# A vision-transformer block on one core: max scores from the spread q and k, and a new order of all engines' work

## What is computed

```python
h = concat([cls_tok, cls_token, patches @ W_lin.T + b_lin])      # 198 rows of 192 per image
# attention: 12 heads of 16, q scaled by 16**-0.5, rotary on q and k
q, k, v = split(layernorm(h) @ w_qkv.T)
h = h + softmax(rope(q * scale) @ rope(k).T) @ v @ w_proj.T + b_proj
# feed-forward: weights ternary, activations rounded to 8 bits after rmsnorm
u = quant(rmsnorm(layernorm(h)) * g_in) @ ternary(w_in).T        # 192 -> 2 * 512
y = silu(gate) * up
h = h + quant(rmsnorm(y) * g_out) @ ternary(w_out).T             # 512 -> 192
```

## Time and profile before

| | us |
|---|---|
| median of 3 runs | 1232.6 |
| lowest and highest run | 1226.38, 1236.34 |
| the profiled execution, its own time | 1228.96 |
| span from the first to the last instruction in it | 1227.2 |
| mean granted clock of TensorE in it | 0.986 |

### The profile page before, as it was taken

One profiled execution on the slowest core, in us unless ns is written; L12 is line 12 of the kernel. 1 busy time (PEld: TensorE's weight loads), 2 busy tenths in 40 slices (PEclk: granted clock), 3 DMA queues, 4 the chain that ended last, 5 costly groups with the idle time before them and its releaser, 6 DMA issues.

```text
span 1227.2 us, 36712 instructions
## 1 busy us (share of the span) xinstructions
PE 1175.8 (96%) x12229; PEld 839.3 (68%) x12229; DVE 960.5 (78%) x2335; ACT 870.0 (71%) x1736; POOL 890.6 (73%) x1605
## 2 busy tenths in 40 slices
PE   6699999999999999999999999999999999999887
PEld 5566766776767767767776776776776776766556
DVE  3455787887788888888888888888888888888786
ACT  1145677777677777777777777777777787778686
POOL 3755687877677787777787777777777788776354
PEclk9889999999899999999999999999999999999899
DMA  7434433443334443444434434344343444322010
GB/s 199 138 94 112 112 95 95 130 117 94 108 96 119 118 120 91 117 127 111 124 89 120 114 99 113 91 130 108 109 122 93 117 122 114 90 80 71 28 50 29
DMA packets 201611, 129.17 MB, mean 105 GB/s; under 512 B 55114, under 2 KB 200725, under 8 KB 201333
## 3 DMA queue, kind: packets, MB, share of 16 engines
q1 hardware_dynamic: 198852, 123.70, 37.2%
q10 hardware_dynamic: 2576, 3.14, 1.0%
HBM read 66.57 MB, written 10.70 MB: 63 GB/s over the span
## 4 chain that ended last, share of the span: by engine, by line
PE 80%; DMA 6%; DVE 5%; ACT 3%; issue 2%; SPq 2%; POOL 2%; ACTq 0%; POOLq 0%; DVEq 0%
PE turn L535 15%; PE score L593 12%; PE turn L615 10%; PE turn L553 10%; PE turn L644 6%; PE score L573 5%; PE turn L602 5%; DMA qkT<-nmaxT 4%; PE turn L623 3%; DVE nmax L935 3%; PE turn L561 2%; PE turn L662 2%; PE turn L624 2%; PE turn L517 2%; PE turn L545 2%
## 5 line engine op out<-in xcount | busy, mean ns | idle before, releaser
L935 DVE TENSOR_REDUCE nmax<-score 99x8 f32<-99x1584 f32 x192 | 347.3, 1809 | 165.3 <-PE score L573 165.3
L744 ACT ACTIVATE prob<-score 99x1584 f32<-99x1584 f32 x192 | 286.4, 1492 | 95.4 <-PE score L593 95.1
L535 PE MATMUL turn<-wlin,xp 128*128 128x192 f32 x1188 | 228.0, 344 | 8.0 <-DMA xp<-in_x 8.0
L535 PEld LDWEIGHTS turn<-wlin,xp 128*128 128x128 f32 x1188 | 198.9, 197 | 18.1 <-issue 8.8
L593 PE MATMUL score<-qkT 32*99 32x198 f32 x3072 | 179.2, 347 | 12.8 <-DVE nmax L935 7.7
L615 PE MATMUL turn<-prob,vaug 99*32 99x198 f32 x3072 | 168.3, 338 | 0.0
L1122 POOL TENSOR_TENSOR yg<-early,gout 128x512 f32<-128x512 f32 x99 | 125.8, 1271 | 46.9 <-ACT yr L808 41.5
L593 PEld LDWEIGHTS score<-qkT 32*99 32x99 f32 x3072 | 116.1, 161 | 56.0 <-issue 39.3
L553 PE MATMUL turn<-wqkv,xT 96*128 96x384 f32 x396 | 151.7, 506 | 0.0
L767 ACT ACTIVATE xiT<-turn 96x256 bf16<-96x256 bf16 x99 | 37.5, 379 | 128.6 <-PE turn L633 128.4
L615 PEld LDWEIGHTS turn<-prob,vaug 99*32 99x32 f32 x3072 | 80.9, 109 | 63.7 <-issue 37.1
(11 more groups left out here) (94 smaller groups left out, 2406.1 us busy)
## 6 DMA issues: line engine op xcount, KB each, us to landing
xp<-in_x SPq DMA_DIRECT2D x63, 588.0 KB, 5.1
qkT<-qkd SPq DMA_DIRECT2D x84, 192.0 KB, 2.5
tab<-joined SPq DMA_DIRECT2D x98, 112.0 KB, 2.7
orec<-rden_kept SPq DMA_DIRECT2D x192, 49.5 KB
out<-h SPq DMA_DIRECT2D x99, 96.0 KB, 3.0
onum<-osb SPq DMA_DIRECT2D x64, 99.0 KB, 2.6
vaug<-vt SPq DMA_DIRECT2D x30, 148.5 KB
onum<-osb SPq DMA_DIRECT2D x64, 49.5 KB, 2.3
```

Of the source, the lines that this page charges most:

```text
L535: last = pe.matmul(turn[:, k, 0:D], xp[:, c, place:place + TILE], wlin[:, c, :], start=(c == 0), stop=(c == KC - 1))
L744: act.activation(prob[:, :, 4 * g:4 * g + 4, :].rearrange("p t r n -> p r t n"), score[0:TT, :, 0:2 * TOKENS].rearrange("p r (t n) -> p r ...
L935: dve.tensor_reduce(nmax[:, b % 2, :, g:HEADS:GROUPS].rearrange("p t r -> p r t"), score[0:TT, :, 0:2 * TOKENS].rearrange("p r (t n) -> p ...
```

## The change

- `max_scores` reads `qkT` itself, seen as fp32r (`bitcast`). `qkTr`, `round_qkT` and its semaphore are gone; TensorE waits for the landing of the last two tiles' `place_qk`.
- The tables: max scores at `2 * final_tile(b) + 10` (the same numbers as before), the output half a step later (`OUT_AT`), projections at `(OUT_AT - 3) // 2`; two labels later in the step lists of what follows them.
- The order of calls in the step is rewritten on all five engines, with other offsets. The weights of the feed-forward are loaded from ACT at `SUM_STEP - 8` = 2 and summed at 8, scaled at 11, rounded at 13 and 14.
- `take` gives `ffn_in` an aligned pair of banks (0 and 1 or 2 and 3).

The unchanged loops and helper functions are as before. The diff, without the removal of `Q_COPIES` and of the semaphore:

```diff
@@ -74,11 +74,11 @@
...
-            top.append(max(top[-1] + 1 if top else 0, 2 * (final_tile(b) + 4) + 2))
+            top.append(max(top[-1] + 1 if top else 0, 2 * final_tile(b) + 10))
         turn.append(top[-1])
         for g in range(GROUPS):
             soft.append(max(soft[-1] + 1 if soft else 0, turn[-1] + 2))
-        out.append(soft[-1] + 7)
+        out.append(soft[-1] + 8)
...
@@ -89,12 +89,12 @@
...
-        steps.append(max(steps[-1] + 1 if steps else 0, (OUT_AT[final_image(i)] + -1) // 2))
+        steps.append(max(steps[-1] + 1 if steps else 0, (OUT_AT[final_image(i)] - 3) // 2))
     return steps
 
 
 PROJ_AT = projection_steps()
-STEPS = PROJ_AT[-1] + 9
+STEPS = PROJ_AT[-1] + 11
...
@@ -196,7 +195,7 @@
...
-        qkTr = sb("qkTr", [128, 2 * GROUPS, QRING], F32R)
+        qkTr = qkT[:, :, :].bitcast(F32R)
...
@@ -335,7 +333,7 @@
...
-        SUM_STEP = 7
+        SUM_STEP = 10
...
@@ -452,30 +450,30 @@
             load(2)
             load(XSLOT)
             for s in range(-1, STEPS):
-                for b in at(OUT_AT, 2 * s + 5):
-                    place_o(b)
-                for b in at(NMAX_AT, 2 * s - 1):
+                for b in at(NMAX_AT, 2 * s):
                     place_max(b)
-                for b in at(OUT_AT, 2 * s + 4):
-                    place_o(b)
-                for i in tile_at(s - 4):
+                for b in at(OUT_AT, 2 * s + 7):
+                    keep_rden(b)
+                for b in at(NMAX_AT, 2 * s + 1):
+                    place_max(b)
+                for i in tile_at(s + 1):
+                    prepare(i)
+                for i in tile_at(s - 3):
                     place_qk(i)
-                for b in at(OUT_AT, 2 * s + 3):
-                    place_rec(b)
                 for i in tile_at(s - 4):
                     place_v(i)
-                for b in at(NMAX_AT, 2 * s):
-                    place_max(b)
                 for b in at(OUT_AT, 2 * s + 5):
+                    place_rec(b)
+                for b in at(OUT_AT, 2 * s + 8):
+                    place_o(b)
+                for i in at(PROJ_AT, s - 10):
+                    store(i)
+                for b in at(OUT_AT, 2 * s + 6):
+                    place_rec(b)
+                for b in at(OUT_AT, 2 * s + 9):
+                    place_o(b)
+                for b in at(OUT_AT, 2 * s + 8):
                     keep_rden(b)
-                for b in at(OUT_AT, 2 * s + 4):
-                    keep_rden(b)
-                for i in tile_at(s + 1):
-                    prepare(i)
-                for i in at(PROJ_AT, s - 7):
-                    store(i)
-                for b in at(OUT_AT, 2 * s + 4):
-                    place_rec(b)
 
             for p in range(TBUF):
                 sp.wait_ge(stored[p], 16 * len(range(p, TILES, TBUF)))
...
@@ -487,7 +485,7 @@
...
-                k = min(range(5 - size), key=lambda n: (max(last_turn[n:n + size]), sum(last_turn[n:n + size])))
+                k = min(range(0, 4, size), key=lambda n: (max(last_turn[n:n + size]), sum(last_turn[n:n + size])))
...
@@ -564,7 +562,8 @@
...
-                pe.wait_ge(qkT_rounded, Q_COPIES[final_tile(b)])
+                for i in range(max(final_tile(b) - 1, 0), final_tile(b) + 1):
+                    pe.wait_ge(qk_placed[i % 2], qk_count(i))
...
@@ -666,46 +665,46 @@
             pe.wait_ge(setup_pool, SETUP_POOL)
             pe.wait_ge(setup_dve, 1)
             for s in range(-1, STEPS):
-                if s == SUM_STEP + 1:
-                    weight_sums()
-                for i in tile_at(s - 3):
-                    project_qk(i)
-                for i in tile_at(s - 4):
-                    transpose_qk(i)
-                for n in at(MAX_AT, 2 * s):
-                    max_scores(n)
-                for n in at(EXP_AT, 2 * s - 2):
-                    weigh_values(n)
-                for i in at(PROJ_AT, s - 2):
-                    ffn_in(i)
-                for n in at(EXP_AT, 2 * s - 1):
-                    weigh_values(n)
-                for n in at(EXP_AT, 2 * s):
-                    exp_scores(n)
-                for i in at(PROJ_AT, s):
-                    project_out(i)
-                for i in tile_at(s - 3):
-                    project_v(i)
-                for i in tile_at(s - 2):
-                    transpose_xn(i)
                 for b in at(NMAX_AT, 2 * s):
                     transpose_max(b)
+                if s == SUM_STEP:
+                    weight_sums()
                 for n in at(MAX_AT, 2 * s + 1):
                     max_scores(n)
+                if s >= TILES + LATE:
+                    keep_busy(s)
                 for i in tile_at(s):
                     embed(i)
                 for i in at(PROJ_AT, s - 7):
-                    ffn_out(i)
-                if s >= TILES + LATE:
-                    keep_busy(s)
-                for i in at(PROJ_AT, s - 1):
-                    transpose_xr(i)
-                for i in at(PROJ_AT, s - 5):
                     transpose_yr(i)
                 for n in at(EXP_AT, 2 * s + 1):
                     exp_scores(n)
+                for i in at(PROJ_AT, s - 8):
+                    ffn_out(i)
+                for i in tile_at(s - 2):
+                    project_qk(i)
+                for i in tile_at(s - 3):
+                    transpose_qk(i)
+                for i in at(PROJ_AT, s - 3):
+                    transpose_xr(i)
+                for n in at(MAX_AT, 2 * s + 2):
+                    max_scores(n)
                 for b in at(NMAX_AT, 2 * s + 1):
                     transpose_max(b)
+                for n in at(EXP_AT, 2 * s):
+                    weigh_values(n)
+                for i in at(PROJ_AT, s - 3):
+                    ffn_in(i)
+                for n in at(EXP_AT, 2 * s + 1):
+                    weigh_values(n)
+                for n in at(EXP_AT, 2 * s + 2):
+                    exp_scores(n)
+                for i in at(PROJ_AT, s - 1):
+                    project_out(i)
+                for i in tile_at(s - 2):
+                    project_v(i)
+                for i in tile_at(s - 1):
+                    transpose_xn(i)
 
         @block.scalar
         def _(act):
...
@@ -834,44 +833,44 @@
 
             act.wait_ge(setup_pool, SETUP_POOL)
             for s in range(-1, STEPS):
-                if s == SUM_STEP - 3:
-                    load_ffn()
-                for n in at(EXP_AT, 2 * s - 1):
-                    copy_o(n)
-                for n in at(EXP_AT, 2 * s):
-                    exps(n)
-                for i in at(PROJ_AT, s - 4):
+                for i in at(PROJ_AT, s - 6):
                     round_y(i)
-                for i in at(PROJ_AT, s - 1):
-                    even_x(i)
-                for i in tile_at(s - 2):
-                    copy_xT(i)
                 for i in tile_at(s - 3):
                     copy_v(i)
                 for b in at(NMAX_AT, 2 * s):
                     copy_maxT(b)
-                for i in at(PROJ_AT, s - 4):
-                    even_y(i)
-                for i in at(PROJ_AT, s - 1):
-                    copy_xiT(i)
-                for i in at(PROJ_AT, s - 5):
+                for i in at(PROJ_AT, s - 3):
+                    even_x(i)
+                for i in tile_at(s - 2):
+                    copy_xT(i)
+                for i in at(PROJ_AT, s - 7):
                     copy_yiT(i)
+                if s == SUM_STEP - 8:
+                    load_ffn()
                 for n in at(EXP_AT, 2 * s + 1):
                     exps(n)
+                for i in tile_at(s - 2):
+                    copy_qk(i)
+                for i in at(PROJ_AT, s - 3):
+                    copy_xiT(i)
+                for i in tile_at(s - 3):
+                    copy_qkT(i)
                 for b in at(NMAX_AT, 2 * s + 1):
                     copy_maxT(b)
-                for i in tile_at(s - 2):
-                    copy_qk(i)
-                for i in tile_at(s - 3):
-                    copy_qkT(i)
-                for i in at(PROJ_AT, s - 2):
-                    sum_squares(i)
                 for n in at(EXP_AT, 2 * s):
                     copy_o(n)
-                for i in at(PROJ_AT, s - 1):
+                for i in at(PROJ_AT, s - 6):
+                    even_y(i)
+                for i in at(PROJ_AT, s - 3):
                     tanh_gate(i)
-                for i in at(PROJ_AT, s):
+                for n in at(EXP_AT, 2 * s + 1):
+                    copy_o(n)
+                for i in at(PROJ_AT, s - 2):
                     round_x(i)
+                for n in at(EXP_AT, 2 * s + 2):
+                    exps(n)
+                for i in at(PROJ_AT, s - 4):
+                    sum_squares(i)
 
         @block.vector
         def _(dve):
...
@@ -1019,46 +1018,46 @@
             dve.memset(qkT[:, 0:GROUPS, :], 0.0).then_inc(qkT_cleared, 1)
             dve.memset(qkT[:, GROUPS:2 * GROUPS, :], 1.0).then_inc(qkT_cleared, 1)
```

(82 more changed lines are left out.)

2 lines of the change are left out of this document (removed).

## The result

The kernel after takes 1275.6 us (median; 1273.6 to 1280.0), the kernel before 1232.4 on the same chip. The ratio is 1.036, 95% interval 1.033 to 1.040: **slower by 43 us**. The forecast was 1216. What came is its rival (a), given a chance of 0.12 and a time of 1275.

What follows compares the result with a forecast made beforehand. TensorE, busy 933.67 of 940 us, was taken to bound the middle, POOL and DMA queues the start. Terms of -6.4, -2.0, -1.7, -1.2, -2, -5, +1, +1 gave -16.3: 1212.7 profiled, 1216 median; range 1202 to 1238.

Steps and rivals of the forecast that it cites:

- rival (a): Middle: den lands 6 us after issue, DVE stands at invert, TensorE loses 60 us: 1275; chance 0.12.
- The term for den: VectorE's invert in the middle: den lands after 4.4 us, with 3.7 plus 0.6 us of room: +1 us.
- The price of a miss: Late den in the middle: TensorE loses 1.7 us for each of 35 even images, 60 us.
- The start: First 60 us and the clock to 69: copy gone -6.4, weight sums moved -2.0, clock -1.7, xn waits -1.2.
- rival (b): Start: second tile's q/k still land at 41; middle: waits for maxima return; 1228, chance 0.28.
- The early weights: Start: weights issued in step 2, not 4, meet SP's image loads, said to have 5 us to spare.
- TensorE's order: Middle: q/k product cheaper behind ffn_out (-7), odd images' transpose_max dearer (+5): net -2 us (-7 to +5).
- The waits for the maxima: Middle: place_max goes first on a quieter queue, so TensorE's waits and clock loss shrink: -5 us (0 to -8.4).
- The feed-forward later: Tail: projections one step later, work moves from start into TensorE's idle time there: +1 us (0 to +3).

Runs made afterwards that it cites:

- e0: Kernel after, but VectorE's reciprocal reads a constant and waits for no den, which is still sent: 1222.2 us, 0.992 of the kernel before.
- e6: Kernel after, den sent ahead of v (even images) or right behind it (odd), VectorE's invert behind quant_y, keep_rden behind place_v: 1246.5 us.
- e4: Kernel after, SyncE sends den and onum ahead of v (even images) or right behind it (odd), ahead of the reciprocals: 1240.3 us.
- e13: Kernel after, den split from onum, sent ahead of v for all images without waiting for onT; onum keeps its place: 1226.6 us.
- e3: Kernel before with only the bitcast and without POOL's copies, every order kept: 1230.2 us, ratio 0.999.
- e8: e6 with the feed-forward weights loaded in step 4 again, as before the change, instead of step 2: 1251.2 us.

## Why the prediction was wrong, step by step

- **The term for den, the step that failed.** The prediction named the place, the mechanism, what is queued behind `invert` and the price of a miss (1275). The term was +1; by e0 it is +53. Two things in it failed. The first is the landing: one value, 4.4 us, where the trace has a spread, median 3.0, every fifth over 5.5 and up to 7.8, and 18 of 51 over the room of 3.7. That q/k and v had had 4 and 2 us to drain was a guess nearer the low end of two bounds; the rows at hand (q/k spread up to 11.7, maxima behind q/k and v 9.4) said that transfers of this queue can land that late. The second is the room. It was worked out for the even images alone, and there it was right: median 3.6 us in the middle, any wait left out. The odd images' den stands last in the step, and the sum gave them nothing, without a reason. Their room is 2.4 us, and they have 13 of the 22 waits and 24.3 of the 51.9 us.
- **The price of a miss** in rival (a) counted 35 equal stalls of 1.7 us, in even images only, and no clock. It was 23 waits of very different length, some 18.6 us of TensorE's idle time, and 30.7 of lower clock. That 1275 was met so closely is luck: 60 us on gains of 17, where 53 us came on gains of 10.
- **The start**: forecast -11.3 (6.4 + 2.0 + 1.7 + 1.2), measured -5.5. First max scores at 39.5, where 36 was forecast with 34.3 to 41.5 as bounds (in e6, e4 and e13 they are at 36.3 to 36.9, with fewer or no microseconds at the lower clock behind the x load). The gain isn't from POOL's copy alone: by e3 the copy at the head of POOL's queue hid the q/k transfer, which takes over at once. The prediction had this as the bound of 41.5, and as half of rival (b). What took most of the rest back are two waits that the forecast did not have, 5.1 us together. Of TensorE up to 110 us, first before, then after:

```profile
PE turn L535 <- DMA xp<-in_x: 8.0, 2, 5.2
PE turn L545 <- POOL xn L1079: 7.6, 4, 6.0
```

```profile
PE turn L533 <- DMA xp<-in_x: 10.4, 3, 5.1
PE score L592 <- DMA qkT<-nmaxT: 2.7, 1, 2.7
PE turn L543 <- POOL xn L1078: 0.5, 1, 0.5
```

The wait for `xn` falls by 7.1 us, that for x grows by 2.4, and the one of 2.7 us for the first maxima is new.

- **The early weights.** I gave the x loads 5 us to spare. The embedding waited 2.59 us for x at 28.66 in the kernel after and 1.02 at 28.12 in e6, and does not in e8, which is e6 with the late load. The Trainium skill (DMA: Bandwidth & Descriptors, Queues, rings and completion order) says that a DMA engine takes turns between the queues that have work for it. The trace agrees with it by that 1.02 us, and so does the q/k transfer's wait of 5.83 us beside the late load in e8.
- **TensorE's order**: net -2 (-7 to +5) forecast, and the middle's work at full clock fell by 4.3 (by 2.8 in e13). The moved `transpose_max` takes 0.26 us to P.V. (523.13 to 523.39) and the q/k product 1.32 behind `ffn_out` (509.55 to 510.87), as forecast from the earlier trace rows.
- **The waits for the maxima**: gone from the middle, as forecast (-5), but that is luck, since den's waits stand in their place. With den in time they are back. From e13's waits of TensorE, 160 to 1100 us:

```profile
PE score L599 <- DMA qkT<-nmaxT: 3.4, 2, 2.5
```

Its idle and clock in the middle are 8.1 and 3.4 us, before 8.0 and 3.4; in e0 they are 6.2 and 1.7. So the term is worth 0 to -3.5.

- **The feed-forward later**: +1 (0 to +3) forecast, the tail is 6.2 us longer, and 4.5 to 5.8 in e13 and e0, which have no late den (135.7 and 137.0 against 131.2). TensorE's work in it grew by 3.3, its idle time by 3.0. The prediction saw that work comes back in the tail and let TensorE's idle time there take it up; in the trace the idle time grew as well.

Put together without den, the forecast change would be -17.3 us on the profiled execution before. e0's profiled execution has -6.8: the start -6.6 where -11.3 was forecast, the middle -6.0 where -7 was, the tail +5.8 where +1 was. (By the medians e0 is 10 us below the kernel before.)
